# Opening of a macaron block: weights' low halves on POOL, whole groups normalised by ScalarE, first tokens over two queues, identity transposes on TensorE

## What is computed

```python
x = x + 0.5 * ffn(layernorm(x))
x = x + attention(layernorm(x))
x = x + 0.5 * ffn(layernorm(x))

# ffn: 16 experts in 4 groups, 4 experts chosen from the 2 best groups
scores = sigmoid(flat @ Wg.T)
topk_idx, topk_w = route(scores, bias_corr)      # topk_w from scores, sum 2.5
hid = relu(einsum('th,eih->eti', flat, W1)) ** 2
y = einsum('eti,ehi->eth', hid, W2)
out = einsum('eth,te->th', y, cw)                # cw: topk_w placed by expert
shared = relu(flat @ Ws1.T) ** 2 @ Ws2.T
```

## Time and profile before

| | |
|---|---|
| median of 3 runs (lowest, highest) | 725.03 us (723.0, 725.87) |
| the profiled execution: its own time, its span | 725.85 us, 724.1 us |
| busy: PE, DVE, ACT, POOL | 685.7, 556.3, 522.3, 403.9 us |
| mean granted TensorE clock | 0.982 of 2.4 GHz |

### The profile page before, as it was taken

How to read it: one execution, slowest core, us unless ns; L and a number is a source line. 1 busy time by engine, 2 the same in 40 slices (tenths; PEclk the granted TensorE clock), 3 DMA queues, 4 the chain that set the end, 5 groups by cost and what they waited for, 6 DMA issues and landing times.

```text
span 724.1 us, 14916 instructions
## 1 busy us (share of the span) xinstructions
PE 685.7 (95%) x3335; PEld 522.5 (72%) x3335; DVE 556.3 (77%) x2586; ACT 522.3 (72%) x1063; POOL 403.9 (56%) x314
## 2 busy tenths in 40 slices
PE   4689999999999997999999999989999999999997
PEld 3467777777777775777777777767777777777775
DVE  5978888788887885666666678978878888788863
ACT  4478788887788866675556667657888788887875
POOL 3377877778777763000000022147787777877874
PEclk9699999999999999999999999989999999999999
DMA  9766776566775650000000000554766777667772
GB/s 250 179 129 127 158 154 142 120 137 148 150 150 119 132 104 0 1 1 1 1 0 0 0 1 1 121 117 92 150 145 148 164 165 166 149 136 173 165 165 68
DMA packets 53525, 78.37 MB, mean 108 GB/s; under 512 B 5216, under 2 KB 19184, under 8 KB 53488
## 3 DMA queue, kind: packets, MB, share of 16 engines
q1 hardware_dynamic: 51280, 77.36, 49.4%
q10 hardware_dynamic: 2208, 0.59, 0.4%
HBM read 72.70 MB, written 5.24 MB: 108 GB/s over the span
## 4 chain that ended last, share of the span: by engine, by line
PE 49%; DVE 21%; ACT 14%; issue 12%; ACTq 1%; POOL 1%; DVEq 1%; DMA 1%; POOLq 0%
PE psum L1189 10%; PE psum L1191 10%; PE psum L1190 9%; PE psum L1398 6%; ACT shared L505 5%; ACT xn L460 4%; PE psum L1220 3%; PE psum L1250 3%; DVE nmax L1069 3%; PE psum L1228 3%; DVE s_sb L939 2%; DVE s_sb L941 2%; DVE bn L747 2%; PE psum L1387 2%; ACT shared L611 2%
## 5 line engine op out<-in xcount | busy, mean ns | idle before, releaser
L379 POOL TENSOR_TENSOR shared_r<-shared,shared_r 128x512 fp32r<-128x512 f32 x224 | 289.0, 1291 | 115.3 <-ACT shared L505 110.3
L939 DVE SCALAR_TENSOR_TENSOR s_sb<-psum,wb 128x512 f32<-128x512 f32 x256 | 176.2, 690 | 75.8 <-PE psum L1191 65.6
L504 ACT ACTIVATE shared_r<-s_sb 128x512 fp32r<-128x512 f32 x224 | 141.3, 631 | 83.0 <-DVE s_sb L939 74.4
L505 ACT ACTIVATE shared<-s_sb 128x512 f32<-128x512 f32 x288 | 178.3, 620 | 21.7 <-DVE s_sb L939 21.4
L1189 PE MATMUL psum<-x_hi,w_hi 128*128 128x512 f32 x288 | 139.3, 484 | 2.7 <-DVE x_sb L1095 2.3
L1191 PE MATMUL psum<-x_hi,w_lo 128*128 128x512 f32 x288 | 115.3, 401 | 0.0
L1190 PE MATMUL psum<-x_lo,w_hi 128*128 128x512 f32 x288 | 114.5, 397 | 0.0
L1189 PE MATMUL psum<-shared_r,w_hi 128*128 128x512 f32 x224 | 97.8, 437 | 0.6 <-POOL shared_r L379 0.4
L1190 PE MATMUL psum<-shared_r,w_hi 128*128 128x512 f32 x224 | 89.2, 398 | 0.0
L1191 PE MATMUL psum<-shared_r,w_lo 128*128 128x512 f32 x224 | 89.0, 398 | 0.0
L362 POOL TENSOR_TENSOR a_rstd<-a_mv,neg_half 128x8 f32<-128x8 f32 x8 | 13.1, 1637 | 116.5 <-DVE a_mv L758 116.5
(11 more groups left out here) (166 smaller groups left out, 1312.1 us busy)
## 6 DMA issues: line engine op xcount, KB each, us to landing
wb<-scratch SPq DMA_DIRECT2D x128, 512.0 KB, 8.4
out<-x_sb SPq DMA_DIRECT2D x16, 256.0 KB, 9.8
x_sb<-in_L_attn_x SPq DMA_DIRECT2D x4, 256.0 KB, 6.2
scratch<-wT SPq DMA_DIRECT2D x32, 32.0 KB, 1.9
w_raw<-in_L_ffn_W ACTq DMA_DIRECT2D x1, 512.0 KB, 5.8
w_raw<-in_L_ffn_W SPq DMA_DIRECT2D x1, 512.0 KB, 6.4
w_raw<-in_L_ffn_Ws ACTq DMA_DIRECT2D x1, 64.0 KB, 8.6
w_raw<-in_L_ffn_Ws SPq DMA_DIRECT2D x1, 64.0 KB, 6.9
```

Source lines behind the costliest of these rows:

```text
L379: nc.gpsimd.tensor_tensor(g_lo[:, j % RING, :], g_f[:, j % RING, :], g_hi[:, j % RING, :].bitcast(F32), ALU.subtract).then_inc(F.glo_done, 1)
L504: nc.scalar.activation(g_hi[:, j % RING, :], s_sb[:, j % RING, :], ACT.Square)
L505: nc.scalar.activation(g_f[:, j % RING, :], s_sb[:, j % RING, :], ACT.Square).then_inc(F.sq_done, 1)
L939: ins = nc.vector.scalar_tensor_tensor(s_, h_, 0.0, wb[:, u, c, :], ALU.max, ALU.mult)
```

## The change

- *Low halves on POOL.* `weights_lo` moves from VectorE's list to POOL's, at four places between its powers. Its source was PSUM; now ACT copies every set a second time, to float32 tiles `wt_f` in SBUF (which lie in zn and oT, unused at this point), and signals after that second copy.
- *Three groups by ScalarE.* For groups 1, 2 and 3 ACT normalises all four tiles (`whole_group`); VectorE only makes the shift.
- *First tokens over two queues.* The first two tiles of group 0 come from SP's queue and the next two from ACT's. ACT then loads the sigmoid's table, waits for both halves, and only then issues W2 and Ws2.
- *Identity transposes.* TensorE transposes the identity 20 times before it waits for Wg, and 12 times before the transposes of group 0. The results are overwritten.

```diff
+        zn_flat = zn[:].rearrange("p u t d -> p (u t d)")
+        wt_f = [zn_flat[:, 512 * w:512 * (w + 1)] for w in range(4)] + [oT[:]]
...
         def _(sp):
-            sp.dma_start(x_sb[:, 0:TG, :], x_v[:, 0:TG, :]).then_inc(x_in[0], 16)
+            sp.dma_start(x_sb[:, 0:TG // 2, :], x_v[:, 0:TG // 2, :]).then_inc(x_in[0], 16)
...
+            def weights_lo(w):
+
+                pool.wait_ge(wt_hi, w + 1)
+                flat = lambda a, k: a[:, 4 * k:4 * k + 4, :].rearrange("p c n -> p (c n)")
+                lo_of = lambda lo, hi, f: nc.gpsimd.tensor_tensor(lo, f, hi.bitcast(F32), ALU.subtract)
+                if w < 2:
+                    lo_of(flat(w1_lo, w), flat(w1_hi, w), wt_f[w]).then_inc(wt_lo, 1)
+                elif w < 4:
+                    lo_of(flat(w2_lo, w - 2), flat(w2_hi, w - 2), wt_f[w]).then_inc(wt_lo, 1)
+                else:
+                    lo_of(w1_lo[:, NC, :], w1_hi[:, NC, :], wt_f[w][:, 0:P])
+                    lo_of(w2_lo[:, NC, :], w2_hi[:, NC, :], wt_f[w][:, P:2 * P]).then_inc(wt_lo, 1)
...
                     if F is FF[0]:
                         x_lo_part(0, 0)
+                        weights_lo(0)
                         norm_root(0)
+                        weights_lo(1)
                         inv(2)
...
                     x_lo_part(1, 1)
+                    if F is FF[0]:
+                        weights_lo(2)
                     inv(3)
+                    if F is FF[0]:
+                        weights_lo(3)
+                        weights_lo(4)
                     norm_root(1)
...
+            sc.dma_start(x_sb[:, TG // 2:TG, :], x_v[:, TG // 2:TG, :]).then_inc(x_in[0], 16)
+
+            sc.wait_ge(const_done, 1)
+            nc.scalar.activation(warm[:], neg_half[:], ACT.Sigmoid)
+            sc.wait_ge(x_in[0], 32)
             sc.dma_start(w2_raw[:, 0:NC, :].rearrange("h c (j i) -> h (c j) i", i=I),
                          W2.rearrange("e h i -> h e i")).then_inc(w2_in, 16)
             sc.dma_start(w2_raw[:, NC, :], Ws2).then_inc(w2_in, 16)
-
-            sc.wait_ge(const_done, 1)
-            nc.scalar.activation(warm[:], neg_half[:], ACT.Sigmoid)
...
+                def whole_group(n):
+                    for t in range(TG):
+                        normalise(F, n, t)
+
                 def opening():
...
-                    first_half(1)
+                    whole_group(1)
...
-                    first_half(2)
+                    whole_group(2)
...
-                    first_half(3)
+                    whole_group(3)
...
                 if w < 2:
-                    copy(flat(w1_hi, w), src).then_inc(wt_hi, 1)
+                    copy(flat(w1_hi, w), src)
+                    copy(wt_f[w], src).then_inc(wt_hi, 1)
...
-                    copy(flat(w2_hi, w - 2), src).then_inc(wt_hi, 1)
+                    copy(flat(w2_hi, w - 2), src)
+                    copy(wt_f[w], src).then_inc(wt_hi, 1)
                 else:
                     copy(w1_hi[:, NC, :], src[:, 0:P])
                     copy(w2_hi[:, NC, :], src[:, P:2 * P])
+                    copy(wt_f[w][:, 0:2 * P], src[:, 0:2 * P])
...
-                        v.wait_ge(x_in[n], 16)
+                        v.wait_ge(x_in[n], 32 if n == 0 else 16)
...
                     statistics(1)
-                    second_half(1)
+                    norm_shift(1)
...
                     route_parts(0, 9)
-                    weights_lo(0)
-                    weights_lo(1)
-                    second_half(2)
+                    norm_shift(2)
                     statistics(3)
                     route_parts(1, 0, 1)
-                    weights_lo(2)
-                    weights_lo(3)
-                    second_half(3)
+                    norm_shift(3)
                     route_parts(1, 2)
-                    weights_lo(4)
...
+                def keep_busy(times):
+
+                    for n in range(times):
+                        nc.tensor.transpose(wt_ps[4][:, 0:P], ident[:], ident[:])
+
                 def opening():
 
                     pe.wait_ge(const_done, 2)
+                    keep_busy(20)
                     pe.wait_ge(wg_in, 16)
                     nc.tensor.transpose(lg_ps[:, 0:E], wg_raw[:], ident[0:E, 0:E]).then_inc(wgT_done, 1)
+                    keep_busy(12)
                     xn_transpose(0, tr_ps)
```

More of the change, by code:

```diff
@@ L724, in _ @@
             v.wait_ge(FF[0].stat, n_const)
[L726 to L737, removed]
             def carry(place):
```

## The result

The changed kernel takes **726.72 us** (median) beside 724.60 for the kernel before on the same chip; the ratio is 1.0027, 95% interval 1.0014 to 1.0039, so 1.0 to 2.8 us more: near the forecast of 726.5, and inside what was called no change (3.6 us), though with this many executions the interval lies clear of 1: the change costs a little. One of the changed kernel's 22 executions took 975.33 us at a mean granted clock of 0.652, and the ratio leaves it out. The profiled execution took 725.45 us with a span of 723.6, which is 0.5 us *less* than the span of before (724.1).

A forecast was written before the change was run, and what follows sets the result against it. The first gate plus an unchanged part was taken to bound the kernel. ACT's delays of +0.4, +0.3 and +0.9 us, less 0.1 returned at the second gate, gave +1.5 on 725.03: 726.5 us, range 723.2 to 729.3.

The forecast's parts named there:

- The serial chain through ScalarE: Opening: 4.9 us more work on ACT delays TensorE's inputs, moving the first gate from 31.25 to 32.85 us.
- the +1.6 at the up product: Group 3's transposes, and TensorE's first up product queued behind them, come 1.6 us later; the product starts at 31.0.
- One sign: ACT in the opening: it was to work without a gap from 11 to 20 us.
- The term for L927: Second gate: VectorE's 0.49 us wait for POOL's power goes, but only 0.1 us is returned.
- The clock: TensorE's opening: identity transposes raise it, group 0's routing comes 1.3 us sooner; group 1's logits run at the lower level.
- Rival 3: Opening: transposes don't raise TensorE's clock, so group 0's routing starts 2.4 us later; 728.6 us, chance 0.13.
- The same puts ACT's first normalisation at 6.9 ... I take 7.3: Start of ACT: behind Ws2's issue its first normalisation comes at 7.3 (was 7.45), so x's 0.8 us gain becomes 0.15.
- rival 2: Start: Ws2's issue holds ACT until W2 lands, first normalisation near 10.4, chain 3.1 us later; 729.6 us, chance 0.09.
- SP's queue ... wb's landing (30.7) moves by no more: SP's queue, held until 19.88 us: wT(0) goes to DRAM, and wb lands, at most 0.4 us sooner.
- rival 1: Opening: TensorE stays at 2.4 GHz, wb's landing sets the gate at 30.4 to 30.8 (-0.4 to -0.8); 723.8 us, chance 0.25.
- Rival 4: TensorE's stall and half clock at 47 to 52 us, some 3.5 us, go; 720.3 us with rival 1, chance 0.05.
- The premise that the time is the first gate plus a constant: Whole kernel: time is the first gate (31.25 us) plus an unchanged part; opening gains count only as that gate moves.

The follow-up runs named there:

- one_queue: Changed kernel with x's first group on SP's queue alone and W2 and Ws2 first on ACT's, as before; ratio to the kernel before 1.0005.
- no_identity: Changed kernel without the 32 identity transposes; ratio to the kernel before 1.0048.
- clock_up: one_queue with 64 more identity transposes in TensorE's later waits of the opening; ratio to the kernel before 0.9995.
- hold_at_49: one_queue with 12 identity transposes in TensorE's wait for group 4's normalised tiles, near 49 us; ratio to the kernel before 0.9985.
- halves_back: Changed kernel with groups 1 to 3 normalised in halves again, VectorE doing tiles 2 and 3; ratio to the kernel before 1.0019.
- low_on_vector: Changed kernel with the low halves on VectorE from PSUM again and without ACT's second copies; ratio to the kernel before 1.0025.
- best: one_queue with identity transposes in all opening waits and at 48 us, x of groups 8 to 15 behind group 1's broadcast; ratio to the kernel before 1.0020.
- ws2_later: Changed kernel with Ws2's issue moved behind group 0's sigmoid; ratio to the kernel before 1.0019.

## Why the prediction was right, and where it was not

*The serial chain through ScalarE* held step by step: routing of group 0 at 11.31 (11.2 forecast), group 1's logits at 14.76 (15.0), wT at 20.38 (20.6), group 2's transposes at 22.34 (22.45), first up product at 30.79 (31.0), gate at 32.55 (32.85), VectorE idle 4.34 us (4 to 5). Of the +1.6 at the up product, +1.38 came. One sign failed without harm: ScalarE was to have no gap from 11 to 20 us, and waited 1.00 and 0.71 us for TensorE at its lower clock (up to 16.69 and 17.62). The term for L927 was mis-sized: I let the second gate give back 0.1 us, and it gave 0.34, so that the chain's price behind it is 0.96 us and not 1.3 (0.7 in one_queue, whose second gate is at 33.48). By G - A, the low halves with their second copies carry 1.1 us and the whole groups 0.55 while POOL holds the low halves.

*The clock* was right in both halves: high for group 0, low for group 1. Rival 3 falls: no_identity shows what it described (logits at 1.86 us, +1.33 us at G - A), and the changed kernel does not. The rule of the Trainium skill behind it ("TensorE: Matmul & The Clock Gate", Part 4) does not hold in these runs: nothing but transposes had run when the clock rose (0.19 us each, then 0.13).

*"The same puts ACT's first normalisation at 6.9 ... I take 7.3"* is the term that was mis-sized. 7.55 was profiled, but four executions of that order average 8.41, 0.9 us later than the old order (7.52 over eight of its profiles). It is rival 2's mechanism, with a smaller price: the issue did not wait for W2's landing (12.1 us, from 3.38 + 8.7) but ended between 7.4 and 8.9 (7.44 in the changed kernel's own profile, just past the 7.4 that was to decide). I had given it 0.09, as an all-or-nothing case at 729.6; it should have been a term of about 1 us in the sum. That the median came out at my number is partly luck. I added 1.5 us to a median of three executions, 725.03; over 22 the kernel before is at 724.60, and the distance is 2.0 us. The chain gave 1.0 of it at most and the hold some 0.9 on average, an estimate from four executions of four kernels; one_queue, without the hold, lies 0.4 us above before (-0.7 to 1.4). Against them stands the clock at 49 us, which differs by execution and not, as far as these runs tell, by the change.

*"SP's queue ... wb's landing (30.7) moves by no more"* than 0.4 sooner was wrong in sign. Qw's issue ended at 19.95, with the two small ones behind it the store went out at 20.94 (20.27 before) and wb at 24.15 (23.04). It cost nothing, since TensorE was later still. But it made rival 1 too cheap: clock_up's gate opened at 31.55, so that -0.4 to -0.8 was +0.3.

*Rival 4*: the stall stayed, as forecast (1.87 us). What I put in one figure, 3.5 us, is a wait that is always there and a fall of the clock that is not; filling the wait gave 1.4 us in hold_at_49.

What stays open: the medians of the changed kernel, halves_back and low_on_vector (1.0019 to 1.0027) cannot be told from each other, so the prices of these two edits rest on one trace each. The price of the hold rests on medians whose intervals overlap a little. The premise that the time is the first gate plus a constant holds only as far as nothing new waits behind it: best opened the gate 2.6 us sooner and gained nothing. What the fall of the clock at 482 to 490 us costs was not measured. Why the length of Ws2's issue varies was not tried, nor was a placing of x's bytes in which no broadcast waits for them.

## What to carry to other kernels

Relieving the busiest engine of an opening pays only up to the next arrival: write down all arrivals at the first full-rate instruction (here routing, up product, broadcast within 0.6 us of each other) before moving work, and charge the engine that receives it with its extra copies. A DMA's issue is work of the engine that issues it and lasted up to 5 us here with over a megabyte asked for ahead of it; put it beside a wait, not behind one. One profile is one execution: when two profiles agree and the medians do not, look for the instruction, or the clock, that varies.

## What was not expected of the hardware

- The issue of Ws2's DMA (64 KB) took 1.76 to 2.78 us when it went out by 1.8 us, and 3.61, 4.41, 4.30 and 5.03 us when it went out at 3.8 to 4.2, with W2 just ahead of it and x, W1 and Ws1 asked for in the other queue. At 10.11 us, in ws2_later, it took 0.35.
- VectorE's pair of 128x128 tiles took 0.60 us alone, 1.23 in before beside one subtraction of POOL, and 2.35 beside two.
- In no_identity the granted clock is recorded as 1.00 in 10 to 15 us while group 0's logits take 1.86 us, the duration of the lower level; the record of a start may not show its true level, and the durations have to be read:
```profile
10.00:15.00 5.00, 4.22 (x19) 3.50 (x18) 1.50 (x13) 2.30 (x7) 0.60 (x1) 1.00 1.11 288
```
